# FFN weight rounding in a fused four-block kernel: clamp and removal of the rounding constant on VectorE in two passes

## The reference

```python
x = x + jnp.tanh(g_xattn[0]) * wkv_recurrence(w, u, layernorm(x), ctx)     # L0 mixing
x = x + jnp.tanh(g_ffn[0])   * ffn_ternary(layernorm(x), w_gate, w_up, w_down)
x = x + jnp.tanh(g_xattn[1]) * cross_attention(layernorm(x), ctx, Wq, Wk, Wv)
x = x + jnp.tanh(g_ffn[1])   * mixture_of_experts(layernorm(x), ...)       # 64 experts, top 8
```

```python
def _quant_weight(w):
    scale = jnp.mean(jnp.abs(w)) + EPS
    wq = jnp.clip(jnp.round(w / scale), -1.0, 1.0)
    return (wq, scale)
```

## Time and profile before

| | before |
|---|---|
| median of 3 runs | 531.2 us (530.32 to 532.62) |
| the profiled execution's own time | 528.41 us |
| its span in the trace | 526.6 us |
| TensorE busy | 406.7 us (77%) |
| VectorE busy | 347.1 us (66%) |
| ScalarE busy | 284.0 us (54%) |
| GpSimd busy | 49.2 us (9%) |
| mean granted TensorE clock | 0.939 of full speed |

### The profile page before, as it was taken

One profiled execution on the slowest core, in us unless ns is written; L12 is line 12 of the kernel. 1 busy time (PEld: TensorE's weight loads), 2 busy tenths in 40 slices (PEclk: granted clock), 3 DMA queues, 4 the chain that ended last, 5 costly groups with the idle time before them and its releaser, 6 DMA issues.

```text
span 526.6 us, 7351 instructions
## 1 busy us (share of the span) xinstructions
PE 406.7 (77%) x2602; PEld 195.1 (37%) x2606; DVE 347.1 (66%) x722; ACT 284.0 (54%) x431; POOL 49.2 (9%) x37
## 2 busy tenths in 40 slices
PE   1101534729668778977799999999999999999994
PEld 1001222315344333433344444444444444444442
DVE  5899599894874664765497567656566565554553
ACT  2855482757785989887655255343343343432321
POOL 0725732001100111000000000000000000000000
PEclk9999955887995999998799999999999999999998
DMA  8400000000001000004530335523333433412211
GB/s 306 165 1 0 1 0 1 1 0 1 0 2 60 1 1 2 2 1 131 151 109 22 111 103 171 183 89 136 128 103 121 139 104 108 131 60 69 71 62 40
DMA packets 24576, 38.01 MB, mean 72 GB/s; under 512 B 4826, under 2 KB 11354, under 8 KB 24028
## 3 DMA queue, kind: packets, MB, share of 16 engines
q1 hardware_dynamic: 24540, 37.54, 22.2%
HBM read 36.21 MB, written 1.31 MB: 71 GB/s over the span
## 4 chain that ended last, share of the span: by engine, by line
PE 58%; DVE 18%; ACT 11%; issue 7%; DMA 2%; POOL 1%; SPq 1%; ACTq 0%; DVEq 0%
PE ps L1140 33%; PE ps L1413 15%; ACT regA L646 3%; DVE regA L801 1%; DVE xn L769 1%; PE ps L1162 1%; PE ps L1197 1%; PE ps L1297 1%; DVE regA L790 1%; PE ps L1340 1%; DMA regA<-in_dp_dram 1%; PE ps L1327 1%; PE ps L1132 1%; ACT regB L551 1%; DMA x<-in_x_dram 1%
## 5 line engine op out<-in xcount | busy, mean ns | idle before, releaser
L1140 PE MATMUL ps<-hH,regB 128*128 128x512 f16 x512 | 164.0, 382 | 0.0
L698 ACT ACTIVATE regA<-ps 128x512 f32<-128x512 f32 x65 | 38.8, 597 | 146.8 <-PE ps L1140 144.9
L1098 DVE TENSOR_TENSOR regA<-ps,regA 128x512 f32<-128x512 f32 x65 | 45.0, 692 | 99.8 <-ACT regA L698 99.8
L1140 PE MATMUL ps<-hL,regB 128*128 128x512 f16 x256 | 97.8, 382 | 0.0
L1413 PE MATMUL ps<-regA,regB 128*128 128x512 f16 x384 | 93.4, 379 | 1.3 <-DVE regA L1103 1.3
L1140 PEld LDWEIGHTS ps<-hH,regB 128*128 128x128 f16 x512 | 50.4, 98 | 61.7 <-issue 2.9
L646 ACT ACTIVATE regA<-ps 128x1024 f32<-128x1024 f32 x64 | 62.0, 1025 | 10.9 <-PE ps L1327 10.0
L1413 PEld LDWEIGHTS ps<-regA,regB 128*128 128x128 f16 x384 | 37.3, 98 | 47.3 <-DVE regA L1103 2.3
L1103 DVE TENSOR_TENSOR regA<-regA 128x512 f16<-128x512 f32 x65 | 44.3, 682 | 0.7 <-ACT regA L690 0.7
L1108 DVE TENSOR_TENSOR regA<-regA 128x512 f32<-128x512 f32 x65 | 44.5, 685 | 0.2 <-DMA regA<-routing_dram 0.2
L690 ACT CAST regA<-regA 128x512 f16<-128x512 f32 x65 | 39.7, 610 | 1.5 <-DVE regA L1108 1.5
(11 more groups left out here) (171 smaller groups left out, 521.8 us busy)
## 6 DMA issues: line engine op xcount, KB each, us to landing
regA<-routing_dram SPq DMA_DIRECT2D x130, 128.0 KB, 3.0
regA<-in_gu_dram SPq DMA_DIRECT2D x32, 256.0 KB, 2.6
regA<-in_dp_dram SPq DMA_DIRECT2D x32, 128.0 KB, 2.7
regA<-in_ffn_dram SPq DMA_DIRECT2D x2, 1024.0 KB, 8.3
x<-in_x_dram SPq DMA_DIRECT2D x2, 512.0 KB, 3.9
ctxT<-in_ctxT_dram SPq DMA_DIRECT2D x1, 1024.0 KB, 8.2
regB<-in_ffn_dram SPq DMA_DIRECT2D x1, 1024.0 KB, 12.3
out_dram<-x SPq DMA_DIRECT2D x2, 512.0 KB, 3.3
```

Source lines behind the costliest of these rows:

```text
L698: nc.scalar.activation(sgm[:, c % 2, :], bank(GATE_BANK[c % 2]), ACT.Silu, scale=UNSCALE).then_inc(esilu_done, 1)
L1098: V.tensor_tensor(sgm[:, c % 2, :], bank(GATE_BANK[c % 2] + 1), sgm[:, c % 2, :], ALU.mult).then_inc(et_done, 1)
L1140: mm = T.matmul(out_ap, w(k), a(k), start=(n == 0), stop=(n == 3 * DK - 1))
```

## The change

The clamp and the removal of MAGIC move to VectorE, as two instructions per matrix: the first subtracts MAGIC and takes the minimum with 1 (f32 in, bf16 out), the second takes the maximum with -1 (bf16, in place). GpSimd's three clamps and ScalarE's three passes go, and so does the semaphore between them. VectorE does matrices 0 and 1 between the normalization of the key rows and `sums(2)`, and matrix 2 between `sums(3)` and `turn_rows(2)`.

```diff
         def _(pool):
-            def clamp(m):
-
-                pool.wait_ge(fz_ready, m + 1)
-                nc.gpsimd.tensor_scalar(fst[m], fst[m], MAGIC + 1.0, MAGIC - 1.0,
-                                        ALU.min, ALU.max).then_inc(fclamped, 1)
-
...
             for c in range(4):
                 differences(c)
-            clamp(0)
-            clamp(1)
             for n in range(2 * TT):
-                if n == HT:
-                    clamp(2)
                 if n not in VECTOR_ROWS:
                     split(n)
...
-            def drop_magic(m):
-                act.wait_ge(fclamped, m + 1)
-                nc.scalar.activation(fw[:, 2048 * m:2048 * (m + 1)], fst[m], ACT.Identity,
-                                     bias=magic[:, 1:2]).then_inc(fw_ready, 1)
...
             turned_integers(0, 2)
-            drop_magic(0)
             split(2)
             split(3)
-            drop_magic(1)
             reciprocal_guess(2)
             project(4, bank(0))
             project(5, bank(1))
-            drop_magic(2)
             reciprocal_guess(3)
...
+            def ternary_weights(m):
+                w = fw[:, 2048 * m:2048 * (m + 1)]
+                dve.wait_ge(fz_ready, m + 1)
+                link(V.tensor_scalar(w, fst[m], -MAGIC, 1.0, ALU.add, ALU.min))
+                V.tensor_scalar(w, w, -1.0, None, ALU.max).then_inc(fw_ready, 1)
+
...
             rows_end(0)
+            ternary_weights(0)
+            ternary_weights(1)
             sums(2)
             turn_rows(0, bank(6))
             turn_rows(1, bank(7))
             sums(3)
+            ternary_weights(2)
             turn_rows(2, bank(6))
             turn_rows(3, bank(7))
             quotient(2)
```

More of the change, by code:

```diff
@@ L200, in bass_flamingo @@
         fz_ready = sem("fz_ready")
-        fclamped = sem("fclamped")
         fw_ready = sem("fw_ready")
```

## The result

The changed kernel takes 534.27 us (median of 20 runs, 530.37 to 537.62), the kernel before 530.36 us (20 runs, 526.64 to 535.58). The ratio is **1.0078, 95% interval 1.0052 to 1.0105**: 0.8% slower, some 4 us. The profiled execution has a span of 532.4 us, where the kernel before had 526.6.

The account below looks back on a forecast made before the run. VectorE, busy from 73.36 us and tied with ScalarE's chain, was taken to set the token loop's start. 5.4 (passes) - 1.7 (clamp(2)) + 0.3 (splits) = 4.0 us on 531.2 gave 535.2 us, range 531.0 to 538.5.

Parts of the forecast that it names:

- Two chains tie, and ScalarE's pass is worth 0: Ahead of ffn_inner(0), ScalarE's and VectorE's chains arrive within 0.1 us, so removing ScalarE's 2.00 us drop_magic(2) gains 0.
- The passes: On VectorE ahead of L835: first pass 1.16 us, second 0.66, 1.8 a matrix, 5.4 us later for three.
- Clamp(2) gives back 1.68: In sums(2), VectorE's L808 regains the 1.68 us it stood beside GpSimd's clamp(2).
- The splits beside the passes cost as much as beside the scans, plus 0.3: From 73.36 us, GpSimd's four splits stall VectorE's passes for 0.3 us more than the 3.55 they cost sums(2).
- The first rival: From 73.4 to 79 us the splits hide under the passes: +0.2 us, 531.4 us in all; chance 0.20.
- The sum: On VectorE ahead of L835: 5.4 (passes) - 1.7 (clamp(2)) + 0.3 (splits) = 4.0 us later.
- the signs named: Expected in the changed profile, among others: sums(2) starting near 80 to 81.5 us, ffn_inner(0) at 104.7.
- It passes through in full: From ffn_inner(0) the token loop is one chain through all engines, so VectorE's 4.0 us delay reaches the end.
- The wait of L495 for L835: Expected sign: ScalarE's square of project(6) waits for VectorE's L835 in place of L467.
- Passes at one column per cycle: Rival: VectorE's passes run at L808's rate, 8.8 us later in all, 540.0 us; chance 0.08.
- The clock rival: The shift changes TensorE's clock at 158 to 173 us: regaining up to 6.3 us, chance 0.04; losing 1 to 2, 0.04.
- The rival's upper figure: The 532.9 us end of the 532.9 to 528.9 forecast if TensorE's clock is regained.

Follow-up runs that it names:

- e1: Kernel before, with only ScalarE's drop_magic(2) moved into ScalarE's idle time ahead of reciprocal_guess(2): 28.79 us to ffn_inner(0), as before; ratio 1.0018.
- e2: Kernel before, with only GpSimd's clamp(2) moved behind clamp(1), into GpSimd's idle time: 1.70 us earlier at ffn_inner(0); ratio 0.9998.
- e3: Changed kernel, with the six passes moved into VectorE's waits between 58 and 67 us: 27.13 us to ffn_inner(0), ratio 0.997 to the kernel before.
- e7: Changed kernel plus three more first passes of matrix 2 behind sums(3): 36.48 us to ffn_inner(0), ratio 1.0119 to the kernel before.
- e9: Changed kernel, with the first expert chunk's two routing-row loads issued ahead of weight pairs 8 and 9: ratio 1.0015 to the kernel before.
- e6: Kernel before, with only matrices 0 and 1 moved to VectorE ahead of sums(2): 3.73 us later at ffn_inner(0); ratio 1.0087.
- e5: Kernel before, with only matrix 2 moved to VectorE behind sums(3): 0.18 us later at ffn_inner(0); ratio 0.9963.

## Why the prediction was right

Predicted were 4.0 us more, 535.2 us on the scale of the runs shown then; measured are +3.91 us in the stretch and a ratio of 1.0078, 4.1 us of 530.4. By its own steps:

- **Two chains tie, and ScalarE's pass is worth 0.** Shown by e1: 0.00 us.
- **The passes.** First 1.16 predicted, 1.23 measured; second 0.66, and 0.69. Which term was too small isn't shown; if the second pass takes just half as long per column as the first, the two durations give 0.53 ns a column and 0.15 us fixed, so it would be the slope (0.484 predicted) and not the fixed part. Both halvings of the estimate hold: the first pass took about half of the 2.27 us that L808's rate would give, and the second, on bf16, about half of the first. The Trainium skill, "VectorE: DVE Perf Modes", section "The perf-mode tier table", has 1227 ns for f32 and 693 ns for bf16; the rows, 1.23 and 0.69 us, agree. One matrix takes 1.87 us (94.49 to 96.36), three 5.6, predicted 5.4.
- **Clamp(2) gives back 1.68.** Shown by e2: 1.70, and by L789 in the changed kernel, 0.69 us where it was 2.37.
- **The splits beside the passes cost as much as beside the scans, plus 0.3.** The mechanism holds, the 0.3 doesn't. In the changed kernel VectorE stands (1.52 - 0.69) + (2.17 - 1.23) + (1.52 - 0.69) + (1.63 - 0.69) = 3.54 us, before it was 3.55. Four stalls each time, one for each split, whatever stands there. The rule of the Trainium skill, "SBUF — State Buffer", section "Who interferes with whom" (one-input instructions in a two-port mode and GpSimd's exclude each other), fits: the passes at 1.23 and 0.69 us alone, in e3 and for matrix 2, take up to 0.94 more beside a split. The first rival, that the splits hide under the passes, falls with this.
- **The sum.** 5.6 - 1.7 + 0.0 = 3.9. The passes' +0.2 and the splits' -0.3 nearly cancel, which is luck, though small beside the 4 us. Of the signs named, sums(2) started at 79.40 us, ahead of the 80 to 81.5 expected, and ffn_inner(0) at 104.28 for 104.7; 0.32 us of each is the earlier arrival at the stretch.
- **It passes through in full.** Up to ffn_inner(0) it does. e7: 3.78 us more for 3 passes that take 3.79 us (94.01 to 97.80). The wait of L495 for L835, named as what takes L467's place, is in the trace with 2.41 us.
- **Passes at one column per cycle** falls with 1.23 us.
- **The clock rival** is not borne out. The profiled execution of the changed kernel did run at full clock near 160 us, where the kernel before had 0.54, but the shift isn't what decides it. In the 15 us from 6 us after ffn_inner(7) the clock was 0.54 in the kernel before and 1.00 in e1, with the same 28.79 us ahead; it was 1.00 in the changed kernel and 0.68 in e9, with the same 32.70 us; and 0.66 in e6, with 32.52. Nor did the higher clock come through to the end. The addition ahead of the first product with the routing rows came 107.82 us after ffn_inner(7) in place of 110.69, 2.9 us earlier, but SyncE issued the load of the rows 107.80 us after it in both kernels, so VectorE waited 4.02 us and the product came 0.9 us later than before. (The rival's upper figure, 532.9, follows from no sum shown with it; 4.0 - 6.3 on 531.2 gives its 528.9.) Of the profiled 5.8 us, 3.9 are the change; the other 1.9 also stand in e1, which is not late (112.93 us from ffn_inner(7) to the first product, then 17.89), so they come without the passes too.

What stays open: why e5, with +0.18 us in the stretch, measures 0.9963. Its loop took 51.40 and its four chunks 16.21 us, so its profile shows nothing of a gain. Its interval ends at 0.9998, and the scatter of single runs (525.6 to 535.6 us for the kernel before) is far wider than that difference; that it comes from where the slow pieces of TensorE's clock fall is likely from the profiles and not shown. I take it as near to no change and did not settle it.

## What to carry to other kernels

A pass named on the chain is worth its length only if no other engine arrives at the same wait within that time: look at the other operand's producer before moving it. Moving work to a faster engine loses when that engine has no gap at that place, even if the work's old home cost it stalls; the same instructions 15 to 30 us earlier in the program, in the same engine's waits, turned +3.9 us into -1.7. And a gain of 1 or 2 us in a latency-bound stretch can vanish in TensorE's clock, so judge such an edit by the distance between two fixed instructions and not by one total.

## What the runs showed of the hardware

- Stalls between VectorE and GpSimd came one for each of GpSimd's instructions (0.77 to 0.94 us for a split that takes 1.16 us alone), whether VectorE ran scans, two-input products or one-input passes in f32 or bf16, and for clamp(2) 1.68 us, on a product as on a scan.
- The token loop had few lengths, 51.4 and 53.6 us, as the start shifted: 51.4 at shifts of 0, +0.2, +3.7 and +3.9 us, 53.6 at -1.7 and 53.7 at +7.7, one profiled execution each. Work that nobody reads in TensorE's waits gave 50.6 once and 53.0 once. Behind the loop the clock did not follow the shift: 0.54 and 1.00 at a shift of 0, 0.68 and 1.00 at +3.9.
